# Edge stage of a four-layer graph network: two staged orders swapped, on TensorE and on VectorE

## The reference, cut to what matters

```python
ip1 = jnp.einsum('eum,eum->eu', p1[edge_dst], p1[edge_src]) / 3.0
s0 = jnp.concatenate([pd0, pd0, ip1], axis=-1)
w = ssp(edge_attr @ W_f1) @ W_f2 * (ssp(s0 @ W_s1) @ W_s2)
w1, w2, w3, w4 = jnp.split(w, 4, axis=-1)
x0e, x1e = split_irreps(x[edge_src])
out0 = w1 * x0e * sh0 + w4 * (einsum('eum,em->eu', x1e, sh1) / sqrt(3))
out1 = w2 * x0e * sh1 + w3 * x1e * sh0
out = segment_sum(merge_irreps(out0, out1), edge_dst, num_segments=N)
```

## Time and profile before

| what | value |
|---|---|
| median of 3 runs | 1556.94 us (1551.32 to 1558.68) |
| profiled execution, its own time | 1552.31 us |
| span of its instructions | 1550.4 us |
| mean granted TensorE clock over the span | 0.927 |
| edge stage, first to last `filters` (L1507) | 884.4 to 1381.5 us of the span |
| busy share of the span | PE 89%, DVE 74%, ACT 50%, POOL 47% |

### The profile page before, as it was taken

How to read it: one execution, slowest core, us unless ns; L and a number is a source line. 1 busy time by engine, 2 the same in 40 slices (tenths; PEclk the granted TensorE clock), 3 DMA queues, 4 the chain that set the end, 5 groups by cost and what they waited for, 6 DMA issues and landing times. The chain is left out here.

```text
span 1550.4 us, 22449 instructions
## 1 busy us (share of the span) xinstructions
PE 1379.4 (89%) x6771; PEld 820.1 (53%) x6771; DVE 1145.0 (74%) x2024; ACT 779.7 (50%) x1997; POOL 733.9 (47%) x768
## 2 busy tenths in 40 slices
PE   5589899899997939999957599999999999985998
PEld 3245577644444539989855344444444444443443
DVE  8977588641206578999936599999999999996023
ACT  2155355300000238979734188878787878761100
POOL 0000399537750357100004588888888888840000
PEclk9889999999998858979878799999999999997999
DMA  8994000000001020500011544444444444401001
GB/s 234 51 113 153 1 2 2 1 8 16 15 11 40 8 113 16 81 1 1 1 37 41 186 140 143 153 152 144 144 150 154 143 147 146 150 25 36 26 14 41
DMA packets 96964, 117.81 MB, mean 76 GB/s; under 512 B 50065, under 2 KB 78225, under 8 KB 96849
## 3 DMA queue, kind: packets, MB, share of 16 engines
q1 hardware_dynamic: 80497, 44.83, 16.5%
q0 software_dynamic: 16352, 71.55, 14.9%
HBM read 96.02 MB, written 11.55 MB: 69 GB/s over the span
## 5 line engine op out<-in xcount | busy, mean ns | idle before, releaser
L431 POOL TENSOR_SCALAR hot_i<-iota_row,il 128x128 f32<-128x128 bf16 x125 | 108.1, 881 | 178.8 <-DVE il L453 172.0
L1426 POOL DMA_INDIRECT far<-far_rows,far_node x150 | 167.6, 1118 | 43.9 <-issue 26.6
L613 POOL DMA_INDIRECT records<-recs,place_i x136 | 137.1, 1008 | 87.4 <-issue 40.9
L1041 PE MATMUL sum_ps<-wx,prob_t 128*128 128x65 f32 x1024 | 140.2, 297 | 12.2 <-DVE prob_t L1073 12.2
L1041 PEld LDWEIGHTS sum_ps<-wx,prob_t 128*128 128x128 f32 x1024 | 138.2, 217 | 13.9 <-DVE prob_t L1073 13.9
L1574 ACT ACTIVATE far<-far,recs 128x128 f32<-128x128 f32 x450 | 138.6, 386 | 0.0
L367 PE MATMUL perm_ps<-hot_high,hot_low 128*128 128x400 f32 x272 | 97.3, 521 | 21.4 <-ACT hot_high L237 21.4
L708 PE MATMUL gcn_ps<-pair,hs 128*128 128x512 f32 x256 | 112.0, 600 | 3.2 <-DVE hs L771 3.2
L1471 PE MATMUL near_ps<-near_parts,hot_t 128*128 x450 | 89.0, 335 | 10.4 <-DVE hot_t L1603 10.4
L1563 ACT ACTIVATE pair<-f_ps,recs 128x256 f32<-128x256 f32 x150 | 72.0, 480 | 51.7 <-PE s_ps L1507 51.7
L777 DVE SCALAR_TENSOR_TENSOR h<-gcn_out_ps,root_p,bias_gcn 128x512 f32<-128x512 f32 x16 | 12.0, 752 | 116.0 <-PE gcn_out_ps L718 116.0
(11 more groups left out here) (332 smaller groups left out, 3272.8 us busy)
## 6 DMA issues: line engine op xcount, KB each, us to landing
pair<-zeros SPq DMA_DIRECT2D x1, 8576.0 KB, 58.5
places<-local_rows SPq DMA_DIRECT2D x75, 64.0 KB, 3.9
s_all<-s_rows SPq DMA_DIRECT2D x8, 512.0 KB, 7.8
records<-empty_record SPq DMA_DIRECT2D x1, 2925.0 KB, 70.7
far<-far_rows,far_node POOLq DMA_INDIRECT x150, 4.7
recs<-in_edge_attr SPq DMA_DIRECT2D x1, 2176.0 KB, 26.8
records<-recs,place_i POOLq DMA_INDIRECT x136, 2.2
w_gcn<-in_L_gnn_W_gcn SPq DMA_DIRECT2D x2, 1024.0 KB, 7.4
```

What stands on the lines that cost most here:

```text
L431: nc.gpsimd.tensor_scalar(hot_i[:, g % 2, k, 1, :], c.iota_row[:], il[:, t + k:t + k + 1], None, ALU.is_equal).then_inc(hot_i_ready, 1)
L613: c.nc.gpsimd.indirect_dma_start(c.rows[:, :], bass.IndirectOffsetOnAxis(ap=c.place_i[:, t:t + 1], axis=0), c.recs[:, t, :], None).then_in ...
L1041: last = nc.tensor.matmul(sum_ps[b % 2][:, h // 4, at:at + DH + 1], prob_t[:, n % PS, k, :], wx[:, k, h, :], start=(k == 0), stop=(k == NB ...
L1426: nc.gpsimd.indirect_dma_start(far[:, u % UNROLL, k, :], None, c.far[:, :], bass.IndirectOffsetOnAxis(ap=far_node[:, t:t + 1], axis=0)) \
```

## The change

Two stages change places in each of two lists, and nothing else changes. On TensorE `add_second` runs ahead of `gather_near`; on VectorE `take_sums` runs ahead of `product`.

```diff
-            staged([(4, filters), (3, turn), (6, add_first), (3, hidden), (1, gather_near), (6, add_second)])
+            staged([(4, filters), (3, turn), (6, add_first), (3, hidden), (6, add_second), (1, gather_near)])
...
-            staged([(4, shift), (2, product), (7, take_sums), (5, messages), (6, block_of), (5, one_hot),
+            staged([(4, shift), (7, take_sums), (2, product), (5, messages), (6, block_of), (5, one_hot),
                     (0, one_hot_turned), (4, weigh)])
```

## The result

| | before | after |
|---|---|---|
| median of 13 runs each, us | 1553.74 (1549.64 to 1558.68) | 1561.01 (1559.5 to 1565.66) |
| profiled execution, its own time, us | 1552.31 | 1560.79 |
| span, us | 1550.4 | 1558.9 |

The ratio is 1.0049, with a 95% interval of 1.0035 to 1.0064: a loss of 5.4 to 9.9 us, 7.3 between the medians. The prediction had 1563.3 us, a loss of 6.4 against 1556.94. That median was of three runs; over 13 it lies 3.2 us lower, so the forecast level lies above the measured one, while the forecast loss lies inside the interval.

What follows compares the result with a forecast made beforehand. TensorE's own work was taken as the bound; +6.7 us over 70 rounds less 0.3 at the stage's end gave +6.4, so the profiled 1552.3 became 1558.7 and, lying 4.6 under the median, 1563.3 us; range 1555 to 1569.

Steps and rivals of the forecast that it cites:

- The bound: Edge stage: TensorE waits for nothing, its own work makes the 6.72 us round; VectorE has at least 0.6 us slack.
- The gap of 0.09 ahead of `filters`: L1525 to `filters`, 0.95 us against 0.86: cost of changing array tile, not waiting for `shift`; it stays.
- The second rival: `filters` waits for `shift` after all, so earlier sums gain up to 0.09 us a round; 1550.6 us if unpaid; chance 0.04.
- The price: L1523 behind `hidden`: exposed fp32 load +0.106 us, bf16 load saved 0.010; +0.096 a round, +6.7 us over 70.
- L1525 to L1471: New succession, second sums to near products on TensorE: taken as 0 us, bounds 0 and 0.09, the tile being unchanged.
- The first rival: At L1523 behind `hidden`: its weights load while `hidden` streams, so the swap costs nothing; 1556.9 us; chance 0.09.
- The register load: L1466, for the near products, moves behind the second sums: its 1.1 us stays hidden under `hidden`, cost 0.
- The third rival: L1466's register load is exposed ahead of the near products: 0.67 us a round, 47 us, time 1610; chance 0.02.
- The rest: VectorE: 0 to 0.3 us wait ahead of `product`, cost 0; GpSimd: `thirds` at most 0.17 earlier, gain 0; stage end: 0.3 back.
- 0.3 was taken: End of the stage, where TensorE waits 0.92 us for `shift`: a VectorE further ahead gives back 0.3 us, bounds 0 and 0.9.
- one of the 70: Rounds 6 to 75, where near products and second sums run together; each was forecast to cost +0.096 us.
- the line of 0.5%: About 0.5%, 7.8 us, taken as what a measurement can tell from no change; the loss was forecast just below it.

Runs made afterwards that it cites:

- the fifth kernel: Both swaps of the change, plus turn's two narrow matmuls moved into `hidden`, against the kernel before: ratio 0.9926, median 1540.93 us.
- the fourth kernel: Order of before, with turn's two narrow matmuls for the next superstep moved into `hidden`, against the kernel before: ratio 0.9917.
- the fifth to seventh: Fourth plus both swaps (0.9926); that with three bf16 near products first (0.9927); that with add_inner's `hot_t` wait replaced by one on `hot_ready` (0.9858).

## Why the prediction was right

**The bound** was right: TensorE's own work. VectorE's half alone left the round at 6.723 us with 0.51 us of waiting in it, and TensorE's half alone gave 6.814.

**The gap of 0.09 ahead of `filters`** was read as a change of tile and not as a wait for `shift`. After, `shift` is over 0.64 us early and the gap stands; and in the fifth kernel the transposes lose 0.10 us where the tile no longer changes behind them. The second rival is out.

**The price** was right in kind and size: 0.106 forecast for the exposed load, 0.104 measured; 0.010 forecast as saved, 0.010 to 0.012 measured; L1525 to L1471 costs no more, as taken. Per round 0.096 forecast, 0.091 measured, which over 70 rounds would be 6.3 to 6.4 us instead of 6.7. The first rival, a hidden load, is out by the load at 1108.79. The sentence of the Trainium skill that was weighed there (TensorE: Matmul & The Clock Gate; it stands under "Architectural detail: the array is 16× 32×32, not 1× 128×128", not under LDWEIGHTS), that loads are pulled ahead of matmuls in flight, held inside the run of full tiles, where L1471's load stands 0.43 us ahead of its matmul, and not behind the narrow ones.

**The register load** stayed hidden: the near products follow L1525 after 0.86 us, which is its streaming time alone. The third rival is out.

**The rest** was sized less well. GpSimd was to gain at most the 0.17 us of idle time ahead of `thirds`. But `thirds` now starts 0.34 us ahead of `filters` (1110.91 against 1111.25), where it stood 0.22 behind (1106.20 against 1105.98). The step that failed took the time of `add_inner` as given. It waits for `hot_t`, which sits behind "firsts" on VectorE, and a shorter "firsts" brings the whole lap forward until `hot_t` has to wait for `hidden`. Nothing came of it, since TensorE waits for none of these. Two rounds at the end, from one `filters` to the next, fell from 7.22 and 6.83 to 6.81 and 6.68 us, giving back 0.56 where 0.3 was taken. In the second of them:

```profile
1383.68 0.70 PE L1507 MATMUL f_ps<-w,soft 32*128 32x512 f32 x2 [0.77 <-DVE soft L1625]
```

That wait was 0.92. The first of the two is one of the 70, so the sum is 69 x 0.091 - 0.56 = 5.7 us, inside the 5.4 to 9.9 measured. The traces agree: the two profiled executions differ by 8.5 us, but 2.5 of that stands already where the first L1517 starts (901.80 instead of 899.34), in the first round in which near products and second sums run together; ahead of it the two kernels run the same instructions in the same order. From there to the last L1517 the difference grows by 5.8 us.

**The chances** gave 0.61 to no change and 0.35 to slower. At a ratio of 1.0049 the result lies on the line of 0.5% that the prediction drew between them. Its interval, 1.0035 to 1.0064, leaves out 1, so 13 runs of each kernel did tell this loss from none; the 7.8 us that the prediction took as the least that can be told was too large.

## What to carry to other kernels

Where an engine is full, an earlier result helps nobody; count what its own list costs in the new order, first of all which instruction stands first behind a change of array tile, since its weight load is exposed: with the 128x128 weights of this kernel some 0.10 us in fp32 and 0.01 in bf16. A recorded wait ahead of such a place proves little: look for another place with the same change whose release came early, and compare the gaps. Once two tile changes were removed, the same swap cost nothing, so the price of an order holds only for the bound that it was measured under.

## What was not expected of the hardware

The two narrow matmuls that moved into `hidden` cost almost nothing there. From L1497 to L1505 it takes 0.61 us (1107.80 to 1108.41) with them, and without them, in the kernel before, L1492 to L1498 takes 0.61 (1109.46 to 1110.07). They write other partitions of `tail_ps` than L1502, start 0.01 us ahead of it (1108.16 and 1108.17), and evidently run beside it. So the edit saves TensorE more than the 0.32 us expected: from the transposes to the second part of the first sums it is 1.14 us in the fifth kernel (1110.45 to 1111.59) instead of 1.68 (1107.05 to 1108.73), which is 0.54 less. As an estimate from these starts, TensorE's own work in the fourth kernel is 6.72 - 0.54 = 6.18 us, not the 6.39 that the fifth to seventh expected.
